# Four graph layers on one core: a stacked inverse transform, two small products moved to GpSimd, and another order of phase three

## The chip, the cores and the metric

The kernel runs on one core of one Trainium2 chip. The metric is the device time of one execution in microseconds (us). An engine is named as the profile names it: PE is TensorE (PEld its weight loads), DVE is VectorE, ACT is ScalarE, POOL is GpSimd, and SP is SyncE, whose queue issues every DMA.

## The reference, cut to what matters

There are 128 graphs of 128 nodes and 128 features, each with a 128 by 128 adjacency matrix. Four layers follow one another, each with a residual and a layer norm at its end. The second is the one that the change is about: a convolution of width 17 along the nodes, messages over learned distances, and a gated recurrent unit.

```python
xc = jnp.transpose(x, (0, 2, 1))
h = relu(bn1(conv1d(xc, conv1_w, 0)))
h = bn2(conv1d(h, conv2_w, 8))                 # 17 taps
x_conv = jnp.transpose(relu(h + xc), (0, 2, 1))
s = x @ w_se.T + b_se                          # 3 codes for each node
A = jnp.exp(-squared_distances(s)) * mask
x_nmp = jnp.einsum('bnm,bmd->bnd', A, relu(x @ w_msg.T + b_msg))
gi = jnp.concatenate([x_conv, x_nmp], -1) @ w_ih.T + b_ih
gh = x @ w_hh.T + b_hh                         # gates r, z, n follow
```

The first layer gathers over the adjacency and has a hidden part of 512 features; the third makes three hops with the row-normalised adjacency; the fourth gathers again and has a hidden part of 256.

## The kernel before

The graphs are worked on in 32 groups of four (`G = 4`), so a tile holds 128 partitions by 4 x 128 numbers and fills one of the eight PSUM banks. There are three phases.

**Phase one** computes the first layer for every group, and the discrete Fourier transform of the second layer's first convolution: 68 frequencies (`SLOTS`), each with a cosine and a sine half, kept in SBUF as `xh`; `wh` holds the transformed taps.

**Phase two** multiplies the two, one frequency after the other: `slot_product` makes three fp32 products for a slot on PE, two slots (a pair) fill a bank, and there are 34 pairs. Even pairs are copied out by ACT and odd ones by DVE into a ring of six tiles (`STAGES`), from which SP stores them to `yh_dram` with at most three stores in flight (`STORES`). POOL negates one half of each slot (`negate`, into `neg_b`). PE may run eight pairs ahead of the copies. The third phase's weights are loaded and split into a high and a low part (`wt_hi`, `wt_lo`) meanwhile.

**Phase three** is a software pipeline that is written out by hand. It has 41 turns (`TURNS3`), and in turn t each engine executes its own list of steps in a fixed order: `stage(step, t - d)` does a step for group t - d if there is such a group. So d is the lag of a step behind the newest group. An engine that waits holds up everything behind it in its list. A step's `until` lines are the semaphores it waits for; PE's `free` lines say which readers must be done with a PSUM bank before it is written again, of which the first that concerns an existing group counts. Since the eight banks are shared by some twenty products, most of the order is about banks.

The steps that matter below are, on PE: `codes` (the points, 16 small products), `distances` (8 small ones), `inverse` (back from 68 frequencies, for each graph one product with 68 rows of cosines and one with 68 rows of sines), `gate_x`, `gate_nmp` and `gate_conv` (each three products of 512 columns in fp32r, high and low parts apart), `hop1` to `hop3`, `y1_t`, `prop_in`, `gather3`, `hidden3` and `down3`. An fp32 product over the four graphs of a group shows as 8 matmul records. On DVE, `agg3` makes `agg3_lo` from the bank that `distances` of the same turn writes next, and `minus_mean` makes minus mean over deviation (`nm`) from 128 x 4 numbers, for `apply2` and `apply3` on ACT. On POOL, `norm` raises 128 x 4 numbers to the power of minus one half. SP's list is `load_x1(t + 2)`, `load_atc(t + 2)`, `load_yh(t + 1)` and `store`; a load waits until the readers of its ring's old entry are done.

The order of PE's turn before is: `codes`, `gather`, `down3` (first half), `messages`, `prop_in`, `down3` (second), `hop3`, `gather3`, `hidden_n`, `gate_x` R and Z, `gate_nmp` R, `distances`, `inverse`, `hop1`, `gate_conv` R, `hidden3` twice, `gate_nmp` N and Z, `gate_conv` N and Z, `y1_t`, `hop2`.

## Time and profile before

| What | us |
|---|---|
| median of 3 runs | 1172.59 |
| lowest and highest | 1169.11, 1173.3 |
| the profiled execution | 1173.6 |
| its span, first to last instruction | 1171.8 |
| PE, DVE, ACT, POOL busy | 1102.7, 833.5, 694.8, 563.0 |

The span is what the rows below divide up. The profiled execution's own time is 1.8 us longer than its span, and 1.0 us above the median. Phase one runs to about 424 us, phase two to about 484, and phase three fills the rest. Merged rows of the timeline overlap a little, as matmuls are pipelined: the distance between the starts of two rows is what a piece of work takes of PE's time.

### The profile page before, as it was taken

How to read it: one execution, taken by the hardware profiler on the slowest of the kernel's cores; microseconds unless marked ns; L12 is line 12 of the kernel's file. 1: busy time of each engine (PE TensorE's matmuls, PEld its weight loads, DVE VectorE, ACT ScalarE, POOL GpSimd, SP SyncE). 2: the span in 40 equal slices, each digit the busy share in tenths (PEclk: the TensorE clock that was granted, in tenths of full speed). 3: DMA queues.
4: the chain of work that ended last, by engine and by line, in shares of the span. 5: the costliest groups of instructions: out<-in, count | busy, mean ns of one | idle time of the engine just before them, and what ended most of it. 6: DMA issues, size and time to landing. Idle time of an engine off the chain costs nothing.

```text
span 1171.8 us, 25210 instructions
## 1 busy us (share of the span) xinstructions
PE 1102.7 (94%) x8267; PEld 990.0 (84%) x8267; DVE 833.5 (71%) x2596; ACT 694.8 (59%) x1296; POOL 563.0 (48%) x524
## 2 busy tenths in 40 slices
PE   7899999999999789899999999999999999999874
PEld 6799999999999679788888888888888888888774
DVE  4477778787777533146887778877787878877974
ACT  4444555555555332256677777767776776767665
POOL 1244433434342235335555555656555565656654
PEclk9999999999999899899999999999999999999998
DMA  4122332223232255411111121211212121220000
GB/s 156 55 64 75 99 91 91 91 91 91 91 91 64 73 168 180 155 50 58 34 40 54 47 65 47 65 38 47 65 47 65 47 65 40 64 65 10 20 28 36
DMA packets 47110, 82.62 MB, mean 71 GB/s; under 512 B 5316, under 2 KB 15368, under 8 KB 46728
## 3 DMA queue, kind: packets, MB, share of 16 engines
q1 hardware_dynamic: 46984, 81.02, 22.5%
q8 instruction: 69, 1.13, 0.4%
q14 instruction: 57, 0.47, 0.1%
HBM read 55.31 MB, written 25.69 MB: 69 GB/s over the span
## 4 chain that ended last, share of the span: by engine, by line
PE 81%; DVE 9%; issue 6%; ACT 2%; DMA 1%; SPq 0%; POOL 0%; DVEq 0%; POOLq 0%; ACTq 0%
PE banks L156 16%; PE banks L465 9%; PE banks L150 9%; PE banks L151 8%; PE banks L152 8%; PE banks L722 4%; PE banks L631 3%; PE banks L632 3%; PE banks L493 3%; PE banks L558 2%; PE banks L609 2%; PE banks L435 2%; DVE stats L1019 2%; DVE prop L1214 2%; PE banks L587 2%
## 5 line engine op out<-in xcount | busy, mean ns | idle before, releaser
L163 POOL TENSOR_TENSOR rstd<-ve,minus_half 128x4 f32<-128x4 f32 x128 | 130.5, 1020 | 101.9 <-DVE ve L1029 98.8
L163 POOL TENSOR_TENSOR r_rms<-ms,minus_half 128x4 f32<-128x4 f32 x32 | 32.3, 1008 | 224.2 <-DVE ms L993 224.2
L465 PE MATMUL banks<-w,s 128*128 128x128 f32 x768 | 101.2, 275 | 0.4 <-DVE y L1007 0.4
L465 PEld LDWEIGHTS banks<-w,s 128*128 128x128 f32 x768 | 95.6, 192 | 3.4 <-issue 0.5
L150 PE MATMUL banks<-agg_hi,w_hi 128*128 128x512 f32 x192 | 82.4, 429 | 10.1 <-issue 8.6
L1373 POOL TENSOR_TENSOR y<-leaky,x_rows 128x512 f32<-128x512 f32 x32 | 42.6, 1331 | 97.3 <-ACT x_rows L922 96.8
L1019 DVE BATCH_NORM_STATS2 stats<-y 128x6 f32<-128x128 f32 x384 | 82.9, 278 | 1.7 <-POOL y L1373 1.6
L1359 POOL TENSOR_TENSOR x3b<-x_rows,late_rows 128x512 f32<-128x512 f32 x32 | 40.9, 1278 | 82.5 <-DVE y L1239 82.5
L160 ACT ACTIVATE agg_hi<-banks 128x512 fp32r<-128x512 f32 x64 | 38.2, 597 | 64.7 <-PE banks L156 36.1
L151 PE MATMUL banks<-agg_lo,w_hi 128*128 128x512 f32 x192 | 76.4, 398 | 0.0
L152 PE MATMUL banks<-agg_hi,w_lo 128*128 128x512 f32 x192 | 76.3, 398 | 0.0
L156 PE MATMUL banks<-at,x_rows 128*128 128x128 f32 x512 | 69.8, 281 | 4.4 <-DVE agg_lo L981 3.0
L156 PE MATMUL banks<-t,atc 128*128 128x128 f32 x512 | 68.8, 278 | 1.3 <-DVE t L1214 1.3
L722 PE MATMUL banks<-w,z 128*128 128x128 f32 x512 | 69.5, 282 | 0.2
L781 ACT ACTIVATE s<-hn,cols 128x512 f32<-128x512 f32 x96 | 65.0, 712 | 7.7 <-DVE hn L1000 7.7
L1000 DVE SCALAR_TENSOR_TENSOR hn<-banks,cols,rv 128x512 f32<-128x512 f32 x96 | 68.2, 736 | 1.0 <-ACT rv L160 0.6
L156 PEld LDWEIGHTS banks<-at,x_rows 128*128 128x128 f32 x512 | 63.9, 196 | 5.3 <-issue 2.9
L722 PEld LDWEIGHTS banks<-w,z 128*128 128x128 f32 x512 | 64.4, 198 | 1.3 <-ACT z L943 1.3
L156 PEld LDWEIGHTS banks<-t,atc 128*128 128x128 f32 x512 | 63.0, 194 | 1.9 <-DVE t L1214 1.9
L1159 DVE SCALAR_TENSOR_TENSOR c_res<-banks,bn_scale,x1c 128x512 f32<-128x512 f32 x32 | 24.0, 751 | 52.0 <-PE banks L632 52.0
L930 ACT ACTIVATE out_rows<-y,nm,rstd 128x128 f32<-128x128 f32 x128 | 52.5, 483 | 11.8 <-DVE nm L1226 11.7
L1315 POOL TENSOR_SCALAR y<-wh 128x128 f32<-128x128 f32 x67 | 34.3, 530 | 47.8 <-ACT xh L160 25.7
(192 smaller groups left out, 3401.1 us busy)
## 6 DMA issues: line engine op xcount, KB each, us to landing
at<-in_at SPq DMA_DIRECT2D x32, 256.0 KB, 2.9
x_rows<-in_x SPq DMA_DIRECT2D x32, 256.0 KB, 2.9
x_scratch<-x SPq DMA_DIRECT2D x32, 256.0 KB, 3.2
ad<-in_ad SPq DMA_DIRECT2D x32, 256.0 KB, 2.7
x1c<-x_scratch SPq DMA_DIRECT2D x32, 256.0 KB, 2.7
atc<-in_at SPq DMA_DIRECT2D x32, 256.0 KB, 2.9
yh<-yh_scratch SPq DMA_DIRECT2D x32, 256.0 KB
out<-out_rows SPq DMA_DIRECT2D x32, 256.0 KB, 3.1
```

Source lines behind the costliest of these rows:

```text
L150: pe.matmul(psum, hi, moving_hi, start=start, stop=False)
L151: pe.matmul(psum, hi, moving_lo, start=False, stop=False)
L152: return pe.matmul(psum, lo, moving_hi, start=False, stop=stop)
L156: last = pe.matmul(psum[:, g, :], lhs(g), rhs(g), start=True, stop=True)
L163: return nc.gpsimd.tensor_tensor(to[:], base[:], minus_half[:], ALU.pow)
L465: last = pe.matmul(bank[7][:, g, :], s[c][:, g, :], w2[:, c, :], start=(c == 0 and g == 0), stop=(c == H0 - 1), skip_group_check=True)
L722: last = pe.matmul(bank[6][:, g, :], z3[c][:, g, :], w32[:, c, :], start=(c == 0 and g == 0), stop=(c == H3 - 1), skip_group_check=True)
L781: nc.scalar.activation(s[c][:], hn[c][:], ACT.Silu, scale=column("rms", c)).then_inc(sem[("s0", "s1", "s2", "s3")[c]], 1)
L930: last = nc.scalar.activation(out_rows[k % OUT_RING][:, g, :], y3[:, g, :], ACT.Identity, bias=nm[1][:, g:g + 1], scale=rstd[3][:, g:g + 1])
L1000: V.scalar_tensor_tensor(out=hn[c][:], in0=bank[(5, 0, 1, 3)[c]][:], scalar=column("b1", c), in1=rv[:], op0=ALU.add, op1=ALU.mult).then_in ...
L1019: last = V.bn_stats(stats[n][:, g, :], y[:, g, :])
L1373: Q.tensor_tensor(y2[:], leaky[:], x2_rows[:], ALU.add).then_inc(sem["y2"], 1)
```

## The change

The **inverse transform** is stacked. The cosines and sines of the first 64 frequencies (`MAIN`) stand in one tile of 128 rows, so that each graph takes one product with 128 rows instead of two with 68. The four frequencies that are left (`REST`, 8 half rows a graph, 32 for the four graphs) are one fp32r product of 512 columns for the whole group: its stationary operand `rest[:, k, :]` stacks high and low parts in four quarters of the partitions, and `rest_idft` holds the matching coefficients.

For that, **phase two** begins with slots 64 to 67. Their two pairs are stored by 16 DMAs, eight a pair, to `rest_dram`; eight times four DMAs (`load_rest`) bring them back into the space of `wt_full`, ACT rounds each eighth (`rest_high`) and DVE subtracts in two quarters (`rest_low`). One more weight is loaded (`rest_idft_full`, 256 KB). The main slots are stored as before. `load_yh` brings the two halves to partitions 0 to 63 and 64 to 127, so its rows are 512 B instead of 1 KB.

**`minus_mean`** leaves DVE for POOL and becomes two instructions there, a negation and a product.

**Phase three** has another order on every engine, other banks, and other lags: the gates' products trail `codes` by two turns instead of one (`gate_x` R stays at one), most of the later steps by one turn more than before, and there are 42 turns. The rings of `x1c` and `atc` have 6 and 11 entries instead of 4 and 8.

Of the order's lists the diff below shows only the new ones.

```diff
-        X1C_RING, ATC_RING, YH_RING, OUT_RING = 4, 8, 2, 2
+        X1C_RING, ATC_RING, YH_RING, OUT_RING = 6, 11, 2, 2
...
-        idft = sb("idft", [SLOTS, 2, P])
+        idft = sb("idft", [P, P])
+        rest_idft_full, rest_idft = sb("rest_idft_full", [P, G * P]), sb("rest_idft", [P, G * P], F32R)
+        rest_full = [wt_full[:, PART * i:PART * (i + 1), :] for i in range(2)]
+        rest = sb("rest", [P, GROUPS, P], F32R)
...
+        SLOT_ORDER = list(range(MAIN, SLOTS)) + list(range(MAIN))
+        NEGATED = [slot for slot in SLOT_ORDER if slot > 0]
+        PARTS = GROUPS // PART
...
+        def stored_pair(engine, p):
+
+            if 0 <= p < REST_PAIRS:
+                engine.wait_ge(rest_stored[p], REST_STORES)
+            elif p >= 0:
+                landed(engine, yh_stored, p - REST_PAIRS)
+
...
-                of_group = yh_dram[:, k * G:(k + 1) * G, :].rearrange("s g (h o) -> s g h o", h=2)
+                of_group = yh_dram.rearrange("s (k g) (h o) -> s k g h o", g=G, h=2)[:, k]
                 to = yh[k % YH_RING]
-                sp.dma_start(to[0:64], of_group[0:64]).then_inc(yh_in[k % YH_RING], 16)
-                sp.dma_start(to[64:SLOTS], of_group[64:SLOTS]).then_inc(yh_in[k % YH_RING], 16)
+                sp.dma_start(to[0:MAIN], of_group[:, :, 0]).then_inc(yh_in[k % YH_RING], 16)
+                sp.dma_start(to[MAIN:P], of_group[:, :, 1]).then_inc(yh_in[k % YH_RING], 16)
...
+                stored_pair(sp, p - STORES)
+                of_pair = spectrum[p % STAGES][:].rearrange("p (s h) o -> p s h o", s=2)
+                slot = SLOT_ORDER[2 * p]
+                if slot < MAIN:
+                    sp.dma_start(yh_dram[slot:slot + 2].rearrange("s b c -> b s c"),
+                                 spectrum[p % STAGES][:].rearrange("p (s a) n -> p s (a n)", s=2)
+                                 ).then_inc(yh_stored[(p - REST_PAIRS) % STORES], 16)
+                else:
+                    for g in range(G):
+                        for s in range(2):
+                            sp.dma_start(rest_dram[g, :, slot - MAIN + s].rearrange("h k o -> k h o"),
+                                         of_pair[g::G, s]).then_inc(rest_stored[p], 16)
+
+            def load_rest(i):
+                if i >= 2:
+                    sp.wait_ge(sem["rest_lo"], 2 * (i - 1))
+                else:
+                    sp.wait_ge(set_dve, DVE_LATE - 1)
+                for r in range(P // (G * REST)):
+                    sp.dma_start(rest_full[i % 2][G * REST * r:G * REST * (r + 1)],
+                                 rest_dram.rearrange("g h s k o -> (g h s) k o")[:, PART * i:PART * (i + 1)]
+                                 ).then_inc(rest_in[i % 2], 16)
...
                 store_slots(p)
+                if p == 8:
+                    for i in range(REST_PAIRS):
+                        stored_pair(sp, i)
+                if p >= 10 and p % 2 == 0 and (p - 10) // 2 < PARTS:
+                    load_rest((p - 10) // 2)
...
                 landed(pe, yh_in, k, 32)
-                free(pe, ("ghn", k - 1), ("y3", k - 8), ("c2_res", k - 1))
+                pe.wait_ge(sem["rest_hi"], k // PART + 1)
+                pe.wait_ge(sem["rest_lo"], 2 * (k // PART + 1))
+                free(pe, ("v", k - 2), ("msg", k - 1), ("z0", k - 9), ("c2_res", k - 1))
+                pe.matmul(flat(bank[7]), rest[:, k, :], rest_idft[:], start=True, stop=False, skip_group_check=True)
                 for g in range(G):
-                    pe.matmul(bank[6][:, g, :], yh[k % YH_RING][:, g, 0, :], idft[:, 0, :], start=True, stop=False)
-                    last = pe.matmul(bank[6][:, g, :], yh[k % YH_RING][:, g, 1, :], idft[:, 1, :], start=False,
-                                     stop=True)
+                    last = pe.matmul(bank[7][:, g, :], yh[k % YH_RING][:, g, :], idft[:], start=False,
+                                     stop=(g == G - 1), skip_group_check=True)
                 last.then_inc(sem["c2_ps"], 1)
...
-            GATE_BANK = {R_GATE: 4, Z_GATE: 7, N_GATE: 0}
+            GATE_BANK = {R_GATE: 1, Z_GATE: 4, N_GATE: 7}
...
                 stage(codes, t)
+                stage(gate_nmp, t - 2, R_GATE)
+                stage(down3, t - 9, 0)
+                stage(messages, t - 1)
+                stage(gate_conv, t - 2, R_GATE)
+                stage(prop_in, t - 5)
+                stage(y1_t, t - 5)
+                stage(down3, t - 9, 1)
+                stage(hidden_n, t - 1)
+                stage(gate_nmp, t - 2, N_GATE)
+                stage(hop2, t - 6)
+                stage(gate_x, t - 2, Z_GATE)
+                stage(gather3, t - 8)
+                stage(gate_conv, t - 2, N_GATE)
+                stage(gate_nmp, t - 2, Z_GATE)
                 stage(gather, t - 1)
+                stage(distances, t)
+                stage(gate_conv, t - 2, Z_GATE)
+                stage(inverse, t)
+                stage(hop3, t - 6)
                 stage(gate_x, t - 1, R_GATE)
+                stage(hop1, t - 5)
+                stage(hidden3, t - 8, 0)
+                stage(hidden3, t - 8, 1)
...
+            def rest_high(i):
+                act.wait_ge(rest_in[i % 2], 16 * 4 * (i // 2 + 1))
+                copy(rest[:, PART * i:PART * (i + 1), :], rest_full[i % 2]).then_inc(sem["rest_hi"], 1)

             for p in range(0, PAIRS, 2):
                 slots_out(p)
+                if p >= 14 and (p - 14) // 2 < PARTS:
+                    rest_high((p - 14) // 2)
                 if p == 6:
...
+                stage(factors, t, 1)
+                stage(hidden3, t - 9, 1)
+                stage(multiple, t - 6, 1)
+                stage(gate_z, t - 3)
+                stage(factors, t, 0)
+                stage(message, t - 1)
+                stage(gate_r, t - 2)
+                stage(gate_n, t - 3)
+                stage(conv_full, t - 1)
+                stage(apply3, t - 10)
+                stage(multiple, t - 6, 0)
+                stage(hidden_n, t - 1)
+                stage(x1_high, t)
+                stage(agg3, t - 8)
+                stage(multiple, t - 5, 3)
+                stage(edges, t)
+                stage(nmp_high, t - 1)
                 stage(conv_high, t - 1)
+                stage(multiple, t - 5, 2)
+                stage(apply2, t - 7)
+                stage(leaky_relu, t - 6)
+                stage(hidden3, t - 8, 0)
...
+            def rest_low(i):
+                dve.wait_ge(sem["rest_hi"], i + 1)
+                for r in (1, 3):
+                    own = slice(G * REST * r, G * REST * (r + 1))
+                    low = rest[own, PART * i:PART * (i + 1), :]
+                    V.tensor_tensor(low, rest_full[i % 2][own], low.bitcast(F32), ALU.subtract
+                                    ).then_inc(sem["rest_lo"], 1)

             for p in range(1, PAIRS, 2):
                 slots_out(p)
+                if p >= 15 and (p - 15) // 2 < PARTS:
+                    rest_low((p - 15) // 2)
                 if p == 7:
...
-            def minus_mean(k, n):
-                until(dve, ("r2", "r3")[n], k)
-                until(dve, ("x3_rows", "out_rows")[n], k - 1)
-                V.scalar_tensor_tensor(out=nm[n][:], in0=mv[2 + n][:, :, 0], scalar=-1.0, in1=rstd[2 + n][:],
-                                       op0=ALU.mult, op1=ALU.mult).then_inc(sem[("nm2", "nm3")[n]], 1)
...
+                stage(twice_n, t - 4)
+                stage(apply1, t - 6)
+                stage(stats2, t - 7)
+                stage(points, t, 0)
+                stage(gate_u, t - 2)
+                stage(stats1, t - 5)
+                stage(moments, t - 7, 2, LN_EPS)
+                stage(moments, t - 5, 1, 4.0 * LN_EPS)
+                stage(points, t, 1)
+                stage(residual3, t - 9)
+                stage(hop, t - 6, 2)
+                stage(scaled_h, t - 5)
+                stage(stats3, t - 9)
+                stage(agg3, t - 8)
+                stage(gate_v, t - 2)
                 stage(nmp_low, t - 1)
                 stage(conv_residual, t)
+                stage(moments, t - 9, 3, LN_EPS)
+                stage(hop, t - 6, 3)
+                stage(twice_x, t - 3)
+                stage(hop, t - 5, 1)
...
+            def minus_mean(k, n):
+                until(pool, ("r2", "r3")[n], k)
+                Q.tensor_scalar(minus_rstd[n][:], rstd[2 + n][:], -1.0, None, ALU.mult
+                                ).then_inc(sem[("minus_r2", "minus_r3")[n]], 1)
+                until(pool, ("minus_r2", "minus_r3")[n], k)
+                Q.tensor_tensor(nm[n][:], minus_rstd[n][:], mv[2 + n][:, :, 0], ALU.mult
+                                ).then_inc(sem[("nm2", "nm3")[n]], 1)
...
+                stage(norm, t - 10, 3)
+                stage(minus_mean, t - 10, 1)
+                stage(residual2, t - 7)
+                stage(add_eps3, t - 8)
+                stage(edge_weights, t - 1)
+                stage(twice_y1, t - 4)
+                stage(norm, t - 5, 1)
+                stage(x1_low, t)
+                stage(norm, t - 7, 2)
+                stage(x3_bias, t - 8)
+                stage(minus_mean, t - 7, 0)
                 stage(conv_low, t - 1)


 def by_group(a):
```

## Rows read from the trace of the kernel before

**Rows 1.** The page's head and its part 1.

```profile
span 1171.8 us, 25210 instructions
...
PE 1102.7 (94%) x8267; PEld 990.0 (84%) x8267; DVE 833.5 (71%) x2596; ACT 694.8 (59%) x1296; POOL 563.0 (48%) x524
```

**Rows 2.** Windows: busy us of each engine, count, clock, DMA share, GB/s.

```profile
1000.00:1100.00 100.00, 97.60 (x729) 86.37 (x728) 81.67 (x289) 71.67 (x138) 59.45 (x50) 1.00 0.14 41
1100.00:1172.00 72.00, 45.90 (x301) 40.75 (x300) 50.08 (x212) 41.65 (x86) 37.25 (x32) 0.89 0.08 30
```

**Rows 3.** Waits of PE, 600 to 1100 us: total, times, longest.

```profile
PE banks L600 <- DVE agg_lo L1232: 14.5, 24, 0.7
```

**Rows 4.** PE timeline, one whole turn: start, length of the merged row.

```profile
1023.03 0.64 PE L587 MATMUL banks<-x1c,code_w 128*32 128x128 f32 x16
...
1032.52 0.39 PE L151 MATMUL banks<-xn_lo,wt_hi 128*128 128x512 f32 x1
1032.75 0.40 PE L152 MATMUL banks<-xn_hi,wt_lo 128*128 128x512 f32 x1
1033.82 0.50 PE L600 MATMUL banks<-points_lr 9*128 9x128 f32 x8 [0.67 <-DVE agg_lo L1232]
1034.25 0.49 PE L631 MATMUL banks<-idft,yh 68*128 68x128 f32 x2
...
1036.14 1.06 PE L156 MATMUL banks<-w3h,atc 128*128 128x128 f32 x8
...
1043.36 0.65 PE L587 MATMUL banks<-x1c,code_w 128*32 128x128 f32 x16
```

**Rows 5.** Groups of 600 to 1100 us: total busy, mean ns.

```profile
L163 POOL TENSOR_TENSOR rstd<-ve,minus_half 128x4 f32<-128x4 f32 x73 | 74.2, 1016 | 48.8 <-DVE ve L1029 48.8
...
L1226 DVE SCALAR_TENSOR_TENSOR nm<-mv,rstd 128x4 f32<-128x4 f32 x50 | 32.8, 656 | 0.0
...
L1214 DVE SCALAR_TENSOR_TENSOR t<-banks,row_inv,w1h 128x128 f32<-128x128 f32 x96 | 27.0, 345 | 0.0
```

**Rows 6.** The page's part 5, the negation on POOL.

```profile
L1315 POOL TENSOR_SCALAR y<-wh 128x128 f32<-128x128 f32 x67 | 34.3, 530 | 47.8 <-ACT xh L160 25.7
```

**Rows 7.** Line 1226 by itself: ns, shortest, median, longest.

```profile
L1226 DVE SCALAR_TENSOR_TENSOR nm<-mv,rstd x64: 143/191/1235, 566.9 to 1167.5; 128x4 f32<-128x4 f32 x64
```

**Rows 8.** PE timeline: first row of turns 0 and 9, of turn 32, and the next.

```profile
485.14 0.65 PE L587 MATMUL banks<-x1c,code_w 128*32 128x128 f32 x16 [1.18 <-DVE prop_w L1138]
...
614.47 0.64 PE L587 MATMUL banks<-x1c,code_w 128*32 128x128 f32 x16
...
1083.76 1.06 PE L156 MATMUL banks<-edge_adj,msg 128*128 128x128 f32 x8
1084.65 1.06 PE L722 MATMUL banks<-w,z 128*128 128x128 f32 x8
```

**Rows 9.** PE and ACT timelines of the last turns.

```profile
1111.29 0.63 PE L672 MATMUL banks<-ident,y 128*128 128x128 f32 x4 [3.54 <-DVE x_rows L1197]
...
1124.85 0.63 PE L672 MATMUL banks<-ident,y 128*128 128x128 f32 x4 [2.45 <-DVE x_rows L1197]
...
1152.70 1.65 ACT L922 ACTIVATE x_rows<-y,nm,rstd 128x128 f32<-128x128 f32 x4 [1.87 <-POOL x3b L1359]
...
1167.68 1.65 ACT L930 ACTIVATE out_rows<-y,nm,rstd 128x128 f32<-128x128 f32 x4 [3.66 <-DVE nm L1226]
```

**Rows 10.** SP's own queue in phase two.

```profile
427.67 0.43 SPq L384 DMA_DIRECT2D msg_w<-in_msg  x1
...
437.71 1.72 SPq L376 DMA_DIRECT2D yh_scratch<-s  x3
```

**Rows 11.** PE and ACT timelines at both ends of phase two.

```profile
424.32 0.46 PE L556 MATMUL banks<-wh,xh 128*128 128x128 f32 x2 [0.58 <-ACT xh L160]
...
483.69 0.27 PE L576 MATMUL banks<-ident,prop_rows 128*128 128x128 f32 x1
...
437.72 0.60 ACT L160 ACTIVATE hn<-banks 128x512 f32<-128x512 f32 x1 [4.17 <-DMA yh_scratch<-hn]
```

More of the change, by code:

```diff
@@ L297, in everything_second @@
             engine.wait_ge(sem["neg_b"], SLOTS - 1)
-            for p in range(PAIRS - STORES, PAIRS):
-                landed(engine, yh_stored, p)
+            for p in list(range(REST_PAIRS)) + list(range(PAIRS - STORES, PAIRS)):
+                stored_pair(engine, p)
         @block.sync
@@ L408, in _ @@
                     stage(load_yh, t + 1)
-                stage(store, t - 9)
+                stage(store, t - 10)
             for i in range(OUT_RING):
@@ L893, in hidden_n @@
                 until(act, "u", k - 1)
-                nc.scalar.activation(ghn[:], bank[6][:], ACT.Identity, bias=half_bhn[:], scale=0.5
+                nc.scalar.activation(ghn[:], bank[2][:], ACT.Identity, bias=half_bhn[:], scale=0.5
                                      ).then_inc(sem["ghn"], 1)
@@ L1327, in _ @@
             Q.memset(pick[:].bitcast(F32), 1.0).then_inc(set_pool, 1)
-            for slot in range(6, SLOTS):
-                negate(slot)
+            for i in range(5, SLOTS - 1):
+                negate(i)
             def x1_low(k):
@@ L1449, in layouts @@
     share = np.where(slot == 0, 1.0, 2.0) / L
+    inverse = waves(node).transpose(1, 2, 0) * share[:, None, None]
+    rest_idft = np.zeros((4, G, REST, G, P), np.float32)
+    for g in range(G):
+        rest_idft[:, g, :, g, :] = inverse[MAIN:].transpose(1, 0, 2).reshape(REST, P)
+    rest_idft = rest_idft.reshape(P, G * P)
     return {
```

225 lines of the change are left out of this document (82 added, 143 removed).

## The prediction

> **What bounds the kernel now.** I read the page's shares first [rows 1]: PE is busy 94% of the span, the others 48 to 71%. The windows by stage then show where that is not so [rows 2]: between 1000 and 1100 us PE is busy 97.60 of 100 us, and in the last 72 us only 45.90. So the middle of phase three goes by PE's own work, the end by latency. PE's waits over 500 us of it hold a single entry [rows 3]: `distances` for `agg3_lo` of DVE, 24 times, 0.60 us each. No load and no other engine stands in that list. The timeline of one turn gives the sizes [rows 4]: a turn takes 1043.36 - 1023.03 = 20.33 us. The last `gate_nmp` product starts at 1032.75 and gives way after 0.23 (the step from the row before it), yet `distances` starts at 1033.82, so 0.84 us pass, some 0.1 to 0.2 of them for changing to small products. I put the wait at 0.70. `inverse` has 1036.14 - 1034.25 = 1.89 us. The 23 turns from turn 9 to turn 31 took (1083.76 - 614.47) / 23 = 20.40 us each, spells of lower clock included [rows 8].
>
> **The change, part by part.**
>
> Inverse transform: for each graph two products of 128 columns become one, and 512 columns in fp32r are added. Four graphs of one fp32 product each take 1084.65 - 1083.76 = 0.89 us [rows 8] and an fp32r product 0.23 [rows 4], so 1.12 instead of 1.89. Some 0.1 of the 1.89 is the lead after the small products, which now falls on another step. I take a saving of 0.67 a turn (0.77 at most; not under 0.5, since eight products leave and five come).
>
> Wait for `agg3_lo`: in the new lists I walked through one turn, with `codes` at 0, PE's pieces back to back at the sizes above, and the other engines' lists at their own durations. The wait was there because `agg3` came late in DVE's list, before a step of PE's middle. Now `gather3` starts at 9.3 and `distances` at 12.5. ACT's high part is done at 11.1. DVE starts `hop` 2 at 8.9 (four pieces of 0.345 [rows 5]), then `scaled_h`, `stats3` and `agg3` follow and end at 12.0. That leaves some 0.3 us. The second tight place is `gather3`, which waits until ACT has copied `ghn` out of its bank: behind `message` (after `messages`, 3.4) stand `gate_r`, `gate_n`, `conv_full`, `apply3` (1.65 us [rows 9]), `multiple` and `ghn`, done at 9.0 against 9.2. Everything else has over 0.5 us: `codes` of the next turn wants `prop` at 19, done at 17.5; `gather` wants `edge_adj` at 11.6, done at 3.3. I remove the whole 0.70 and put 0.12 back for the two tight places, between nothing and 0.75. The turn is 20.40 - 0.67 - 0.70 + 0.12 = 19.15 us. ACT and DVE, 14.5 and 16.5 us of work a turn [rows 2], fit in it.
>
> `minus_mean`: DVE loses two instructions a turn, 0.656 us in the mean [rows 5], though it waits for PE anyway. The same line takes 0.143 to 1.235 us [rows 7]; a length so unequal for 512 numbers is waiting within the instruction. The Trainium skill, page "SBUF — State Buffer", section on its two separate sides, says that VectorE with two SBUF inputs and GpSimd hold a shared port pair by turns, for a whole instruction. By that rule the trace agrees, and moving work to GpSimd blocks other DVE steps (`twice_n`, `twice_x`, `gate_u`) in its place. From rows, one such block costs 1.235 - 0.143 = 1.1 us; two at the head of DVE's list delay `points` and `gate_u`, but `hop` 2 still starts about when PE delivers, since DVE idled before it. POOL gains four small instructions a turn. The trace has none like them: below stands 0.14, DVE's own [rows 7], above the power on as many numbers, 1.02 [rows 5]. The negation of 128 x 128 in 0.53 [rows 6] is nearest, and I take 0.5. POOL then has 12.1 + 2.0 us of a turn (59.45 over 100 us are 12.1 [rows 2]), so this costs nothing in the middle. In the drain it lies on the path (below). The Trainium skill, page "GPSIMD Engine Reference", section 3.1, speaks against the move: VectorE stays the rule for elementwise work, GpSimd being 1.96 times as slow. Worked out from that ratio, an estimate is 0.28 an instruction, by which the sum below would be some 2 us less.
>
> Phase two: PE's work is the same, (483.69 - 424.32) / 34 = 1.75 us a pair [rows 11]. The first negation is needed a little earlier: 0.3 us. SP has 14 more stores at the start and one more weight load, at 0.43 to 0.57 each [rows 10] 7 us. Pair 6 was copied at 437.72, after a store had landed [rows 11]. PE had it ready at 436.5 and wants its bank for pair 14 at 448.8. So the copy may be some 10 us later, and the stores hide there; with that cover gone each us counts (0 to 5). The 32 `load_rest` DMAs take SP 15 us over the 14 pairs that last 24.5, beside 8 for stores, and the handshakes lag by some 3 us behind copies that have six tiles. The extra copies on ACT (0.6) and DVE (two of 0.7) a second pair lie in their gaps.
>
> Rings: SP's loads no longer wait for readers of the same turn. No PE wait was a load's, so nothing. `load_yh` has as many DMAs as before.
>
> Fill: before, turns 0 to 8 took 614.47 - 485.14 = 129.3 us [rows 8]. Since the gates now come two turns behind, the early turns are lighter. With fp32 steps at 0.89, fp32r ones at 0.70, `codes` 0.67, `distances` 0.53, `messages` 1.12, the turns are 7.5 and 8 (latency), three of 10.6, 12.8, two of 14.6, and 16.9: 106.2 us, 23 less.
>
> Drain: the same work comes back here. Before, from 1083.76 to the end 88.0 us. After, turn 32 has 19.0 less `codes`, `distances` and `inverse`, 16.6; turn 33 also lacks `messages`, `hidden_n`, `gather` and `gate_x`, 13.2. Then a chain sets the pace: `y1_t`, statistics, two powers, `x3b`, two small POOL instructions, `apply2`, `leaky_relu`, `hidden3`, `down3`. I add it up to 11.5 us, three times (before, 1124.85 - 1111.29 = 13.6 [rows 9]), then 9 and 7.1 to the end of the last `apply2`. From there it took 1171.8 - 1154.4 = 17.4 [rows 9]; with the small instructions 18. Sum 98.4, 10 more.
>
> **Sum**: 485.4 + 106.2 + 23 x 19.15 (440.5) + 98.4 = 1130.5 of span; with the 1.8 us around it 1132.3. The profiled execution, 1173.6, is 1.0 above the median, so **1131** for the median of runs.
>
> **The rivals.**
>
> The wait moves: one of the two tight places, or one I misjudged, costs 0.75 us a turn, as `agg3_lo` did. Over 31 turns 0.63 more than I put back is 20 us: 1151. For it: three tenths of a us are less than my walk can promise, and shared-port blocks fall on DVE. Against: only the excess over the slack counts.
>
> Fill and drain better than I add up: if the drain stays at its old 88 us and no tight place costs (3 us), 1118. Against it: two more steps on POOL, and one more turn.
>
> Phase two stalls: stores or `load_rest` fall behind PE by more than the ten us of cover, 5 to 10 us: 1139. Against it: the queue catches up in 3 us after its worst wait before.
>
> The other side: POOL becomes the bound. The small instructions would have to cost over (20.4 - 12.1) / 4 = 2.1 us each to bring the turn back to 20.4 and the time to about 1172, and 2.3 would give some 1190. The power on as many numbers, 1.02, speaks against it. Only twice that decides.
>
> **How the numbers follow.** Forecast as summed 0.58, the wait moves 0.22, better ends 0.09, phase two 0.05, POOL 0.06. The predicted time is 1131. The range 1114 to 1160 leaves out POOL and the worse half of the moved waits. Under 0.5% (6 us) this kernel's runs can't be told from no change; the first four cases are all faster by more, save the far tail of the second: faster 0.89, same 0.05, slower 0.06.
>
> **What would show it.** `inverse` as one fp32r product and four fp32 ones, 1.1 us in all. The starts of `codes` 19.0 to 19.3 us apart, and no wait at `distances`; waits at `gather3` for `ghn` or at `distances` for `agg3_lo` would be the second case. The small POOL instructions near 0.5 us. No PE idle time in phase two. Turn 9 starting near 592, turn 32 near 1032. The prediction is wrong if PE idles over 0.5 us a turn at any place, or if phase three's last ten turns take over 110 us.

## The result, and the profile after

The changed kernel took 1131.81 us in the median of four runs (1130.30 to 1132.04), the kernel before 1170.85 in the same comparison. The ratio is 0.9655, with an interval of 0.9628 to 0.9682. The forecast was 1131 us. The profiled execution took 1131.74 us, with a span of 1129.9. The forecast had taken the profiled execution to lie 1.0 us above the median, as it did before; it lay 0.1 below it.

The page's head and part 1 after, against [rows 1]:

```profile
span 1129.9 us, 24862 instructions
...
PE 1074.6 (95%) x8043; PEld 961.1 (85%) x8043; DVE 818.6 (72%) x2549; ACT 709.2 (63%) x1305; POOL 613.6 (54%) x652
```

PE has 224 matmuls and 28 us of busy time less, but the span shrank by 42, so 14 us of PE's idle time went as well. The windows after, against [rows 2]:

```profile
600.00:800.00 200.00, 200.00 (x1508) 175.67 (x1507) 161.33 (x576) 156.12 (x293) 142.11 (x148) 1.00 0.17 54
800.00:1000.00 200.00, 200.00 (x1515) 175.44 (x1514) 162.36 (x577) 158.05 (x298) 142.32 (x148) 1.00 0.17 55
...
1060.00:1100.00 40.00, 32.00 (x229) 28.62 (x230) 36.35 (x157) 29.26 (x57) 28.74 (x34) 0.96 0.06 21
1100.00:1130.00 30.00, 14.52 (x93) 11.65 (x91) 13.39 (x61) 15.65 (x34) 16.20 (x24) 0.92 0.12 44
```

From 600 to 1000 us PE is busy for the whole of both windows; before, the 100 us in the middle of [rows 2] had 97.60. The list of PE's waits between 590 and 1030 us is empty; from 600 to 1100 us before it had 24 of them at 0.60 us [rows 3]. In 1060 to 1100 us it is DVE that is nearly full: 36.35 of 40 us.

One turn of PE's timeline after, against [rows 4]:

```profile
802.59 0.64 PE L637 MATMUL banks<-x1c,code_w 128*32 128x128 f32 x16
...
811.90 1.05 PE L160 MATMUL banks<-at,x_rows 128*128 128x128 f32 x8
...
815.18 0.50 PE L650 MATMUL banks<-points_lr 9*128 9x128 f32 x8
...
816.41 0.39 PE L682 MATMUL banks<-rest_idft,rest 128*128 128x512 f32 x1
816.65 1.05 PE L684 MATMUL banks<-idft,yh 128*128 128x128 f32 x8
817.53 1.06 PE L160 MATMUL banks<-t,atc 128*128 128x128 f32 x8
...
821.52 0.65 PE L637 MATMUL banks<-x1c,code_w 128*32 128x128 f32 x16
```

A turn is 821.52 - 802.59 = 18.93 us. `inverse` is the fp32r product and four fp32 ones, 817.53 - 816.41 = 1.12 us. `gather3` starts 9.31 us into the turn and `distances` 12.59, as the walk through the lists had it (9.3 and 12.5).

The turn that [rows 4] shows is not quite a typical one. More first rows of turns before, and two windows of 3 us:

```profile
634.70 0.64 PE L587 MATMUL banks<-x1c,code_w 128*32 128x128 f32 x16
...
656.68 0.65 PE L587 MATMUL banks<-x1c,code_w 128*32 128x128 f32 x16
...
921.85 0.65 PE L587 MATMUL banks<-x1c,code_w 128*32 128x128 f32 x16
...
942.09 0.64 PE L587 MATMUL banks<-x1c,code_w 128*32 128x128 f32 x16
...
648.00:651.00 3.00, 3.00 (x13) 2.71 (x12) 1.93 (x6) 2.18 (x4) 2.52 (x3) 0.50 0.20 79
791.50:794.50 3.00, 3.00 (x13) 2.71 (x12) 1.79 (x6) 2.18 (x4) 2.52 (x3) 0.50 0.24 72
```

Of the 22 distances between the first rows of turns 9 to 31, 15 are 20.21 to 20.24 us, five are 20.27 to 20.38, and two are 21.98 and 21.99. In each of these two turns the granted clock fell to 0.50, that is 1.2 GHz, for a few microseconds (last column but two of the windows), at a cost of 1.75 us. A clean turn before is therefore 20.24 us, and the mean of 20.40 that the prediction started from holds 0.16 of slower and disturbed turns.

The first rows of turns 0, 9 and 31 and the first `down3` of turn 32, against [rows 8]. Turn 32 has no `codes`; it starts at 1010.85 + 18.93 = 1029.78:

```profile
485.30 0.64 PE L637 MATMUL banks<-x1c,code_w 128*32 128x128 f32 x16 [1.27 <-DVE prop_w L1209]
...
594.36 0.65 PE L637 MATMUL banks<-x1c,code_w 128*32 128x128 f32 x16
...
1010.85 0.65 PE L637 MATMUL banks<-x1c,code_w 128*32 128x128 f32 x16
...
1030.39 1.05 PE L774 MATMUL banks<-w,z 128*128 128x128 f32 x8
```

So phase three divides into a fill (turns 0 to 8), 23 full turns (9 to 31), of which the table has the mean, and a drain. The same division serves for every experiment, from the profile of each; it leaves phases one and two out, whose end wanders between 483.4 and 489.9 us from profile to profile.

| Kernel | phase three | fill | one turn | drain |
|---|---|---|---|---|
| before | 686.7 | 129.3 | 20.40 | 88.0 |
| forecast | 645.1 | 106.2 | 19.15 | 98.4 |
| changed | 644.6 | 109.1 | 18.93 | 100.1 |
| changed, second profile | 643.9 | 109.1 | 18.93 | 99.4 |
| 1: new order, old inverse | 665.6 | 115.6 | 19.59 | 99.4 |
| 2: old order, stacked inverse | 660.0 | 122.3 | 19.61 | 86.7 |
| 3: old kernel, `agg3` earlier | 670.5 | 128.6 | 19.59 | 91.4 |
| 4: old order, stacked, `agg3` earlier | not read | | | |
| 5: `minus_mean` on DVE | 648.0 | 109.2 | 18.93 | 103.4 |
| 6: POOL's two steps swapped | 644.8 | 109.3 | 18.93 | 100.1 |
| 7: another order in the last turns | 648.0 | 109.6 | 18.93 | 103.0 |
| 8: `agg3` later | 651.7 | 109.7 | 19.22 | 100.1 |
| 9: `ghn` later | 656.1 | 111.3 | 19.35 | 99.8 |
| 10: shorter rings | 645.0 | 109.4 | 18.93 | 100.1 |
| 11: as 4, `agg3` earlier in the middle only | 643.2 | 121.0 | 18.93 | 86.8 |

The profiled execution of experiment 4 had a mean granted clock of 0.56, against 0.98 to 0.99 in all the others, and its times compare with none of them.

### The profile page after: what moved, and what is told of

Read it like the earlier page. It is cut to its first block, busy times and chain, and to the rows that moved or that the text cites. A ratio compares the mean times of both kernels' runs of the same rounds, so it can differ in the third digit from the quotient of the medians.

```text
span 1129.9 us, 24862 instructions
## 1 busy us (share of the span) xinstructions
PE 1074.6 (95%) x8043; PEld 961.1 (85%) x8043; DVE 818.6 (72%) x2549; ACT 709.2 (63%) x1305; POOL 613.6 (54%) x652
## 4 chain that ended last, share of the span: by engine, by line
PE 89%; DVE 4%; issue 3%; POOL 2%; ACT 1%; DMA 1%; SPq 0%; ACTq 0%; DVEq 0%; POOLq 0%
PE banks L160 18%; PE banks L154 12%; PE banks L155 10%; PE banks L156 10%; PE banks L515 10%; PE banks L774 4%; PE banks L684 3%; PE banks L543 3%; PE banks L608 3%; PE banks L659 2%; PE banks L485 2%; PE banks L637 2%; PE banks L575 1%; PE banks L611 1%; PE banks L613 1%
## 5 line engine op out<-in xcount | busy, mean ns | idle before, releaser
L1420 POOL TENSOR_TENSOR y<-ya,yb 128x512 f32<-128x512 f32 x32 | 41.6, 1299 | 63.2 <-PE banks L724 62.5
L1406 POOL TENSOR_TENSOR x_lo<-x1c,x_hi 128x512 fp32r<-128x512 f32 x32 | 41.2, 1287 | 62.7 <-ACT x_hi L164 62.7
L1223 DVE TENSOR_TENSOR xn_lo<-banks,xn_hi 128x512 fp32r<-128x512 f32 x32 | 22.1, 692 | 60.4 <-ACT xn_hi L164 60.4
L1387 POOL TENSOR_SCALAR y<-wh 128x128 f32<-128x128 f32 x67 | 38.0, 585 | 44.4 <-ACT xh L164 25.7
L1426 POOL TENSOR_TENSOR xc_lo<-xc,xc_hi 128x512 fp32r<-128x512 f32 x32 | 41.1, 1285 | 34.0 <-issue 17.5
```

The costliest lines, as they stand in the source:

```text
L1406: Q.tensor_tensor(x1_lo[k % 2][:], x1c[k % X1C_RING][:], x1_hi[k % 2][:].bitcast(F32), ALU.subtract).then_inc(sem["x1_lo"], 1)
L1420: Q.tensor_tensor(y1[:], ya[:], yb[:], ALU.subtract).then_inc(sem["y1"], 1)
```

## The experiments

Times are medians of four runs or more, and each ratio is to the kernel before in runs on the same chip. Experiments 1 to 4 ran on one chip, 5 to 7 with the changed kernel again on a second, 8 to 10 on a third, and 11 on a fourth, so across these sets the ratios compare better than the times.

### 1. The new order with the old inverse transform

Everything of the change but the stacked transform and its part of phase two:

```diff
-                pe.matmul(flat(bank[7]), rest[:, k, :], rest_idft[:], start=True, stop=False, skip_group_check=True)
                 for g in range(G):
-                    last = pe.matmul(bank[7][:, g, :], yh[k % YH_RING][:, g, :], idft[:], start=False,
-                                     stop=(g == G - 1), skip_group_check=True)
+                    pe.matmul(bank[7][:, g, :], yh[k % YH_RING][:, g, 0, :], idft[:, 0, :], start=True, stop=False)
+                    last = pe.matmul(bank[7][:, g, :], yh[k % YH_RING][:, g, 1, :], idft[:, 1, :], start=False,
+                                     stop=True)
```

> The changed kernel, with the inverse transform and phase two of before (two products of 68 rows for each graph, no rest), on the new order and banks. Theory (PE's own work sets the turn): the turn grows from 18.93 by the 0.67 us of the products, 32 times 21 us, so about 1153 us, turns 19.6 us apart, no PE wait in the middle. Rival (the new order alone made the gain, the products lay in its slack): 1132 to 1137 us. Rival (phase two's extra stores and loads cost something that this gives back): below 1149 us.

Measured: 1152.69 us, ratio 0.9824 (0.9795 to 0.9854). Turns of 19.59 us, and PE waits for nothing from 600 to 1000 us. The drain is 99.4 us. With the old transform the new order still has no wait, so its 11 longer us of drain belong to the order and not to the transform.

### 2. The old order with the stacked transform

The other half: the kernel before with the stacked transform, its phase two and its extra loads, nothing else.

> The kernel before, with the stacked inverse and its phase two only; order, banks, lags, rings and minus_mean as before. Theory (PE's own work sets the turn, and the wait at distances lies ahead of the inverse in the turn): 0.67 us a turn less, 21 us in all, about 1150 us; the wait for agg3_lo stays at 0.6 us, the turn goes from 20.24 to 19.57. Rival (a cycle through DVE sets the turn and the wait grows by what is saved): 1166 to 1171 us, wait over 1.0 us.

Measured: 1150.17 us (1144.42 to 1151.61), ratio 0.9792 (0.9758 to 0.9826). PE's waits from 600 to 1000 us keep one entry, as [rows 3] had:

```profile
PE banks L650 <- DVE agg_lo L1303: 12.5, 21, 0.7
```

It is 0.60 us a turn, as before, with turns of 19.61 in the mean and 19.57 in the median. The transform is worth 0.67 us a turn here (20.24 less 19.57, clean turns on both sides). In the new order it is worth 19.59 less 18.93, 0.66. So its worth doesn't hang on the order around it.

Phase two takes 59.6 us from its first product to the one behind its last, here as in the changed kernel, and 59.4 before. PE has no wait within it. With 14 stores more at its head and 32 `load_rest` DMAs, SP kept up.

### 3. The old kernel with `agg3` earlier on DVE

One step moved by two places, in a list of the kernel before:

```diff
+                stage(agg3, t - 7)
                 stage(minus_mean, t - 6, 0)
                 stage(stats3, t - 8)
-                stage(agg3, t - 7)
```

> The kernel before with one line moved: on DVE agg3 stands ahead of minus_mean and stats3 instead of behind them. Theory (the wait was only a matter of agg3's place in DVE's list): agg3_lo is done some 1.6 us earlier, the wait at distances goes, 0.6 to 0.7 us in some 25 turns, so 15 to 17 us less, about 1155 us, turns of 19.6 us. Rival (another wait of PE takes its place, since stats3 and the points now come later): 1166 to 1171 us.

Measured: 1157.81 us, ratio 0.9869 (0.9845 to 0.9894). The turns are 19.59 us and the wait is gone, so it cost 20.24 less 19.59, 0.65 a turn. But the drain grew from 88.0 to 91.4 us. In the last turns `agg3` now goes ahead of `minus_mean` and waits for ACT first:

```profile
1126.83 0.69 DVE L1232 TENSOR_TENSOR agg_lo<-banks,agg_hi 128x512 fp32r<-128x512 f32 x1 [0.27 <-ACT agg_hi L160]
1127.44 0.15 DVE L1226 SCALAR_TENSOR_TENSOR nm<-mv,rstd 128x4 f32<-128x4 f32 x1
```

That this is what lengthens the drain is tested in experiment 11.

### 4. Both

> Both: the kernel before with the stacked inverse and with agg3 moved ahead on DVE. Theory (the new order buys that one wait and no more, and shifts work from the fill to the drain without gain): 21 and 16 us add up, about 1134 us, within 4 us of the changed kernel; turns of 18.9 us. Rival (with shorter turns the old order has further waits that only the new one avoids): 1140 to 1155 us, with PE waits in the middle.

Measured: 1138.57 us, ratio 0.9697 (0.9666 to 0.9727). The 4.6 us over the 1134 expected are about the drain's 3.4 of experiment 3. By the ratios (0.9697 here, 0.9655 and 0.9677 of the changed kernel, with intervals that overlap) one step moved and the new transform have all but 2 to 5 us of what the change has. What then do the new order, its lags, banks and rings give?

### 5. `minus_mean` back on DVE

```diff
         @block.vector
+            def minus_mean(k, n):
+                until(dve, ("r2", "r3")[n], k)
+                until(dve, ("x3_rows", "out_rows")[n], k - 1)
+                V.scalar_tensor_tensor(out=nm[n][:], in0=mv[2 + n][:, :, 0], scalar=-1.0, in1=rstd[2 + n][:],
+                                       op0=ALU.mult, op1=ALU.mult).then_inc(sem[("nm2", "nm3")[n]], 1)
...
                 stage(gate_u, t - 2)
+                stage(minus_mean, t - 10, 1)
...
+                stage(minus_mean, t - 7, 0)
                 stage(conv_residual, t)
```

The two steps of the same name are taken out of POOL's list.

> The changed kernel with minus_mean back on DVE as one instruction (behind gate_u for group t - 10, ahead of conv_residual for group t - 7). Theory (it is off PE's path in the middle, and in the drain it costs DVE about what it cost POOL): 1130 to 1135 us, turns still 18.93. Rival (a block of up to 1.2 us by POOL on each of the two eats the small slack ahead of distances and gather3): PE waits come back, 1140 us or more.

Measured: 1136.21 us, ratio 0.9697 (0.9669 to 0.9724); the changed kernel in the same comparison 1132.13, ratio 0.9677 (0.9650 to 0.9705). The intervals overlap. The middle is the same, 18.93. The profile has a drain of 103.4 us against 100.1 and 99.4, and its timeline from 1100 us to the end says from what:

```profile
1108.22 2.05 PE L774 MATMUL banks<-w,z 128*128 128x128 f32 x16 [1.18 <-ACT z L1002]
...
1109.76 0.42 DVE L1297 SCALAR_TENSOR_TENSOR nm<-mv,rstd 128x4 f32<-128x4 f32 x1
...
1110.22 1.65 ACT L989 ACTIVATE out_rows<-y,nm,rstd 128x128 f32<-128x128 f32 x4 [1.47 <-DVE nm L1297]
...
1114.29 0.76 PE L154 MATMUL banks<-agg_hi,w_hi 128*128 128x512 f32 x1 [2.89 <-issue]
...
1115.88 1.24 DVE L1297 SCALAR_TENSOR_TENSOR nm<-mv,rstd 128x4 f32<-128x4 f32 x1 [1.13 <-POOL rstd L167]
...
1116.99 3.50 PE L774 MATMUL banks<-w,z 128*128 128x128 f32 x16
```

The same place in the second profile of the changed kernel:

```profile
1106.28 2.05 PE L774 MATMUL banks<-w,z 128*128 128x128 f32 x16 [1.10 <-ACT z L1002]
...
1106.70 1.64 ACT L989 ACTIVATE out_rows<-y,nm,rstd 128x128 f32<-128x128 f32 x4
...
1110.92 0.47 PE L154 MATMUL banks<-agg_hi,w_hi 128*128 128x512 f32 x1 [1.46 <-ACT agg_hi L164]
```

In DVE's list `nm` stands behind the statistics of another group, so `apply3` (`out_rows`) starts 2.00 us after `down3` instead of 0.42. `residual3` and `agg3_lo` come later with it, and PE is idle for 2.89 us ahead of `hidden3` instead of 1.46. That is 1.4 us of the edit's own cost. The rest is the clock: right behind that idle time the granted clock is 0.50, and the next `down3` takes 3.50 us where the others take 2.05. Whether the longer idle time brought the lower clock isn't shown. DVE also stands idle 1.13 us before `nm` while POOL makes its power, three times in the last turns.

The runs don't confirm a cost. The four runs of this kernel with a mean clock of 0.984 to 0.991 and the five of the changed one with 0.986 to 0.992 agree once they are put side by side by clock: at 0.986, 1136.05 and 1136.38 us against 1135.59 and 1135.79; at 0.991, 1131.97 against 1131.96 and 1132.13. So the move to POOL is worth between nothing and some 1.4 us, all of it in the drain, and no gain clear of the noise is shown.

### 6. POOL's `minus_mean` ahead of `x3_bias`

```diff
-                stage(x3_bias, t - 8)
                 stage(minus_mean, t - 7, 0)
+                stage(x3_bias, t - 8)
```

> The changed kernel with minus_mean ahead of x3_bias in POOL's list. Theory (in the last turns the chain to apply2 passes x3_bias, 1.27 us): the middle is the same, the last five turns or so get shorter, 2 to 5 us less, about 1128 us. Rival (DVE, busy 91% there, sets those turns): under 1 us.

Measured: 1131.72 us, ratio 0.9663 (0.9641 to 0.9685), so no gain. The rows of one of the last turns:

```profile
1101.68 0.20 POOL L1367 TENSOR_TENSOR nm<-minus_rstd,mv 128x4 f32<-128x4 f32 x1
1101.83 1.27 POOL L1431 TENSOR_TENSOR x3b<-x_rows,late_rows 128x512 f32<-128x512 f32 x1
...
1103.22 1.65 ACT L981 ACTIVATE x_rows<-y,nm,rstd 128x128 f32<-128x128 f32 x4 [2.17 <-POOL x3b L1431]
```

`nm` is there at 1101.88, 1.3 us before ACT starts `apply2`, and `apply2` now waits for `x3b` instead. There is a single tile of `x3_rows`: it can't be written before `x3_bias` has read the group before. I had overlooked that reader. Both orders have the same two steps ahead of `apply2`.

### 7. Another order in the last turns

This is the kernel of experiment 6, with POOL's two steps swapped, and with one thing more: in turns 39 to 41 (`LAST` is 39) PE does `gather3` first, and ACT and DVE do `agg3` before `multiple` and `residual3`. PE's and DVE's part, against the changed kernel:

```diff
+                if t >= LAST:
+                    stage(gather3, t - 8)
                 stage(codes, t)
...
-                stage(gather3, t - 8)
+                if t < LAST:
+                    stage(gather3, t - 8)
...
+                if t >= LAST:
+                    stage(agg3, t - 8)
                 stage(residual3, t - 9)
```

> As the one before, and in the last three turns gather3 ahead of down3 on PE and agg3 earlier on ACT and DVE. Theory (group 31's gather3 stood 2.5 us behind down3 of group 30): another 2 us less, about 1126 us. Rival (the last chain goes by other steps): no change against the one before.

Measured: 1135.24 us, ratio 0.9696 (0.9670 to 0.9723), no gain over experiment 6 (1131.72, 0.9663), and by the profile's drain (103.0 us against 100.1) a loss. The rows:

```profile
1111.76 1.24 ACT L1006 ACTIVATE z<-banks,cols 128x512 f32<-128x512 f32 x2
1111.77 1.26 POOL L1447 TENSOR_TENSOR at<-atc,eps_ident 128x512 f32<-128x512 f32 x1
...
1113.14 1.13 PE L160 MATMUL banks<-at,x_rows 128*128 128x128 f32 x8 [1.96 <-issue]
1114.11 3.44 PE L775 MATMUL banks<-w,z 128*128 128x128 f32 x16
...
1121.55 1.65 ACT L993 ACTIVATE out_rows<-y,nm,rstd 128x128 f32<-128x128 f32 x4 [1.73 <-POOL nm L1377]
1123.32 0.69 DVE L1311 TENSOR_TENSOR y<-banks,x3b 128x512 f32<-128x512 f32 x1 [3.53 <-ACT out_rows L993]
```

`down3` has its input soon after ACT starts the first `z`: in the second profile of the changed kernel it starts 0.72 us behind it (1113.68 and 1112.96). Here it starts 2.35 us behind, at 1114.11, because `gather3` now stands ahead of it in PE's list and waits for POOL's `at`. So the edit costs 1.6 us on the chain at this point. Another 1.4 us are that `down3` at a lower clock, which again comes right behind idle time of PE. What `gather3` gains is lost: `agg3` is done early, but the last `residual3` waits for `apply3` of the group before, which must have read the one tile `y3`, and that `apply3` comes from the `down3` that was put off. By clock, its run at 0.991 took 1133.26 us against 1131.96 and 1132.13 of the changed kernel, and the one at 0.986 took 1135.52 against 1135.59 and 1135.79. So by the runs the edit costs about 1 us at most, and gains nothing.

### 8. `agg3` behind `gate_v` on DVE

```diff
-                stage(agg3, t - 8)
                 stage(gate_v, t - 2)
+                stage(agg3, t - 8)
```

> The changed kernel with agg3 behind gate_v on DVE, so 0.6 us later. Theory (0.3 to 0.4 us of slack there, as the prediction had it): a PE wait of 0.2 to 0.35 us before distances comes back in every full turn, 6 to 10 us in all, about 1139 us. Rival (the slack is larger than read, or the wait is made up elsewhere in the turn): no change.

Measured: 1137.59 us, ratio 0.9709 (0.9676 to 0.9742). The turn is 19.22 us, 0.29 more, for a step that holds DVE 0.6 us ahead of `agg3_lo` (in the changed kernel `agg3_lo` starts at 813.82 and the step behind it at 814.41). So `distances` had some 0.3 us to spare. PE's waits from 600 to 1000 us:

```profile
PE banks L650 <- issue: 4.5, 21, 0.4
```

The wait is back at the same product, `distances`, though the profile names no engine for it.

### 9. ACT's `ghn` later

A copy of a whole tile that nobody reads is put before `hidden_n` on ACT:

```diff
+            def idle_copy(k):
+                copy(unused[:], wt_full[:, 0:G, :])
+
...
+                stage(idle_copy, t - 1)
                 stage(hidden_n, t - 1)
```

> The changed kernel with one more ACT copy of a full tile (0.6 us, into a tile that nobody reads) ahead of the copy of ghn. Theory (0.2 to 0.3 us of slack before gather3): PE waits 0.3 to 0.6 us before gather3 in every full turn, 9 to 18 us in all, about 1145 us. Rival (ACT makes it up, or gather3's bank is released in time): no change.

Measured: 1140.61 us, ratio 0.9726 (0.9694 to 0.9759). From turn 10 on the turns are 19.37 us, 0.44 longer, and the copy puts `ghn` off by 0.52 us (it starts at 819.15, `ghn` at 819.67), so `gather3` had only 0.1 to spare. PE's waits from 610 to 1000 us name the one that the prediction named:

```profile
PE banks L160 <- ACT ghn L957: 4.2, 20, 0.2
```

They are 0.21 us each, less than the 0.44, since idle time counts from the modelled end of the row before, and PE's rows overlap: in the changed kernel the row ahead of `gather3` starts at 811.67 and is 0.40 long, while `gather3` starts at 811.90.

### 10. Rings of 5 and 9

```diff
-        X1C_RING, ATC_RING, YH_RING, OUT_RING = 6, 11, 2, 2
+        X1C_RING, ATC_RING, YH_RING, OUT_RING = 5, 9, 2, 2
```

> The changed kernel with rings of 5 and 9 entries for x1c and atc instead of 6 and 11. Theory (loads have a turn to spare, so that SP may wait for readers of the same turn): no change, 1132 us. Rival (SP, held up by atc's readers into the next turn, issues yh too late): PE waits for yh before inverse, 1140 us or more.

Measured: 1130.93 us, ratio 0.9654 (0.9620 to 0.9687): no difference, with turns of 18.93 and no wait in the middle. Entries above 5 and 9 are worth nothing. Whether the new lags would run well with the old 4 and 8 wasn't tried.

### 11. The old order, stacked transform, `agg3` earlier in the middle only

Experiments 3 and 4 lost in the drain what `agg3` ahead of `minus_mean` costs there. So the step is moved only while there are new groups, in the kernel of experiment 2:

```diff
+                if t < GROUPS:
+                    stage(agg3, t - 7)
                 stage(minus_mean, t - 6, 0)
                 stage(stats3, t - 8)
-                stage(agg3, t - 7)
+                if t >= GROUPS:
+                    stage(agg3, t - 7)
```

> The kernel before with the stacked inverse, and agg3 moved ahead on DVE in the first 32 turns only; in the last nine it stands where it stood. Theory (the old order with these two edits runs its middle at 18.93 us a turn as the changed kernel does, and its drain stays at 88 us or so): turns of 18.93 us without a PE wait, 1133 to 1136 us. Rival one (a wait of the old order remains in the middle): turns of 19.1 us or more, 1138 us or more. Rival two (the early agg3 did not lengthen the drain): the same time as with agg3 ahead in all turns, 1138.6 us, and a drain of over 90 us.

Measured: **1129.86 us** in the median of five runs (1128.91 to 1131.29), ratio 0.9640 (0.9624 to 0.9656), the changed kernel having 0.9655 (0.9628 to 0.9682) and 0.9677 (0.9650 to 0.9705) in its two comparisons. Its windows:

```profile
600.00:800.00 200.00, 200.00 (x1519) 175.50 (x1518) 161.93 (x595) 154.11 (x297) 125.57 (x107) 1.00 0.19 57
800.00:1000.00 200.00, 200.00 (x1499) 174.88 (x1498) 162.81 (x590) 153.93 (x297) 125.78 (x106) 1.00 0.19 55
...
1060.00:1100.00 40.00, 27.62 (x188) 24.96 (x187) 34.34 (x144) 25.49 (x52) 23.21 (x20) 0.91 0.06 21
```

Here, too, PE has no idle time in 400 us, and the turn is 18.93 us, the same as the changed kernel's to the hundredth. The fill is 121.0 us instead of 109.1 and the drain 86.8 instead of 100.1, in all 643.2 us against 644.6. It is at least as fast as the changed kernel, from two edits. Against experiment 4 (0.9697, 0.9666 to 0.9727) the intervals don't touch, and the two differ in the last nine turns alone: so it was the earlier place of `agg3` in these turns that lengthened the drain in experiments 3 and 4.

## Why the prediction held, step by step

The sum was 1130.5 us of span and 1129.9 was measured. The terms were not that good: their errors cancel, start -0.1, fill +2.9, the 23 turns -5.1, drain +1.7. What held is the mechanism, PE's own work and one wait in the middle and a shift from fill to drain; that the sum came within a microsecond is luck.

**The turn.** Forecast 20.40 - 0.67 - 0.70 + 0.12 = 19.15 us, measured 18.93. This is the term that was most off, 5.1 us over 23 turns. Against the clean turn of 20.24 us, experiment 3 gives 0.65 for the wait, put at 0.70, and experiments 2 and 1 give 0.67 and 0.66 for the transform, put at 0.67. The two terms that were mis-sized are others. The start of 20.40 held 0.16 of slower turns, most of it the two spells of 1.2 GHz, that the changed kernel's middle doesn't have. And the 0.12 put back for tight places cost nothing. Together these are 0.28 a turn, less 0.05 for the wait. From 600 to 1000 us of the changed kernel the granted clock was 1.00 throughout, while the kernel before had 0.98 in two windows of 100 us. Why it had such spells is open: experiment 2, with the wait still there, also has 1.00 in these windows, so the wait doesn't bring them every time.

**The two tight places.** Both are where the forecast had them. The timeline of all engines in the turn shown above:

```profile
810.94 0.68 ACT L953 ACTIVATE ghn<-banks,half_bhn 128x512 f32<-128x512 f32 x1
...
813.82 0.67 DVE L1297 TENSOR_TENSOR agg_lo<-banks,agg_hi 128x512 fp32r<-128x512 f32 x1
```

`ghn` is done at 811.62 for a `gather3` at 811.90, and `agg3_lo` at 814.49 for `distances` at 815.18. The delays of experiments 8 and 9 give what was to spare: 0.3 us at `distances` and 0.1 at `gather3`, less than the 0.69 and 0.28 between these ends and starts. They also show what the rival, the wait moving, would have cost: half a microsecond on one engine made phase three 7 and 11 us longer. It was a close thing, and a chance of 0.22 was not too much.

**`minus_mean` on POOL.** The four small instructions were put at 0.5 us each; they are shorter. Groups from 600 to 1000 us, of the changed kernel:

```profile
L1437 POOL TENSOR_TENSOR at<-atc,eps_ident 128x512 f32<-128x512 f32 x21 | 36.5, 1736 | 0.0
...
L1257 DVE SCALAR_TENSOR_TENSOR yb<-tz,nn 128x512 f32<-128x512 f32 x21 | 25.6, 1219 | 0.0
L1364 POOL TENSOR_SCALAR minus_rstd<-rstd 128x4 f32<-128x4 f32 x42 | 16.4, 391 | 1.8
...
L1367 POOL TENSOR_TENSOR nm<-minus_rstd,mv 128x4 f32<-128x4 f32 x42 | 8.4, 200 | 3.5
```

They are 0.39 and 0.20, 1.2 us a turn in all instead of 2.0, far from the 2.1 each from which POOL would have been the bound. That it costs nothing in the middle held. The small loss put on the drain isn't there: the part behind the last `apply2`, put at 18 us instead of 17.4, took 17.2 (from 1112.7). The profile of experiment 5 points the other way, since on DVE the step stands behind others and cost 1.4 us. That was not foreseen.

**Blocks between DVE and POOL.** The prediction expected new ones at the head of DVE's list. There is one pair: `yb` takes 1.219 us (before 0.692) and `at` 1.736 (before 1.335). One turn shows how:

```profile
802.03 1.29 POOL L1445 TENSOR_TENSOR y<-leaky,x_rows 128x512 f32<-128x512 f32 x1
...
802.66 1.21 DVE L1257 SCALAR_TENSOR_TENSOR yb<-tz,nn 128x512 f32<-128x512 f32 x1
...
803.28 1.74 POOL L1437 TENSOR_TENSOR at<-atc,eps_ident 128x512 f32<-128x512 f32 x1
```

`yb` starts while POOL's `y` runs, stays until that is over at about 803.3, and then needs its own 0.5 to 0.6; `at` starts at 803.28 and is 0.40 longer than before. So they take turns, each for a whole instruction. By the rule of the Trainium skill, page "SBUF — State Buffer", section on the two separate sides, which gives the shared port pair to one of them for an instruction at a time, the trace agrees. It is not `minus_mean`'s doing: with `minus_mean` back on DVE (experiment 5) `at` still takes 1.740 us and `yb` 1.029, and in experiment 11, which has the old order, 1.285 and 0.694. The new order brings the two together, for in experiment 1, with the old transform, they take 1.216 and 1.733. Since DVE has time to spare in the middle, it costs nothing there. What the prediction took as evidence for such blocks, `nm` of 0.656 us on DVE, also went with the order alone: 0.153 us in experiment 5.

**Fill.** 109.1 us against 106.2. Half of the miss is turn 5, forecast at 12.8 and measured at 14.3: `distances` waits in it, once.

```profile
543.58 0.50 PE L650 MATMUL banks<-points_lr 9*128 9x128 f32 x8 [1.22 <-issue]
```

It is the first turn with the steps of lag five. Turn 4 took 0.9 us more than forecast (0.48 of it one wait for `msg`) and turn 1 took 1.0 less. The rest is 0.2 us in each of the six others, probably from changes between product forms, which I had left out in summing single pieces; no run shows that.

**Drain.** 100.1 us against 98.4. The three turns that I put at 11.5 us took 12.2, 13.2 and 11.0; what follows them, put at 9, 7.1 and 18, came out 0.6 us shorter. A spell of 1.2 GHz from 1081 us on is in the second of the three; the second profile, with the same waits of PE around it (1.05 and 0.90 us) and no such spell, has 12.2, 12.0 and 11.5 and a drain of 99.4. The chain was the one described, but in these turns DVE's load counts as well as latency: 36.35 of 40 us.

**Phase two.** Nothing, as forecast: the phase ends at 483.75 us and `codes` starts at 485.30, before 483.69 and 485.14 [rows 8, 11].

**What the parts are worth.** Stacked transform: 26.7 us of phase three by itself, 686.7 to 660.0, of which 3.5 are the two spells of lower clock before; the medians of the runs, 1173.80 and 1150.17 us, are 23.6 apart. The wait: 16.8 more, 660.0 to 643.2, with one DVE step in another place. The rest of the new order, the lags, the banks, the longer rings and `minus_mean` on POOL: minus 1.4, between profiles that differ by 0.7 when one kernel is profiled twice. This rest makes the fill 11.9 us shorter and the drain 12.6 to 13.4 longer. That it is the longer lags that do this is argued, from the steps that each early and late turn holds; no run changes the lags alone. The prediction saw this give-and-take (23 less in the fill, 10 more in the drain) but laid the 23 to the lags and lighter products together; 8.3 of the 20.2 us that were measured come with the old lags too, as experiment 11 shows.

## What to carry to other kernels

In a pipeline in which one engine is full, an engine's own work and its single repeated wait are the whole gain in the middle; find the one step whose place causes the wait and move that before a new order is written, for here the rest of the new order only made the fill shorter and the drain longer by about as much. Give the steady turns and the last turns orders of their own where a step that helps the one stands on the other's chain. Before a step is moved to shorten a chain, list all readers of the tile that it lets be written, since in experiment 6 a tile with one copy took the gain, and list what then stands behind the step in its own engine's list, since in experiments 3, 5 and 7 that was a step of the chain.

## What the runs showed of the hardware

Within the runs of one kernel, the mean granted clock of each run goes with most of what differs: in the five runs of the changed kernel in the second comparison 1130.5 us went with 0.992, 1132.0 and 1132.1 with 0.991, 1135.6 and 1135.8 with 0.986. That is some 0.7 us for each thousandth of clock here; from 0.985 to 0.995 the runs of experiment 10 give 0.5. So edits of a few microseconds are best compared at about equal clocks. It is a rough scale: two runs of the kernel before at 0.986 took 1169.81 and 1171.75 us. The lower clock showed up within single products of the drain, 16 `down3` matmuls in 3.44 us instead of 2.05 in experiment 7, where PE had been idle for 1.96 us just before the eight products ahead of them, and 3.50 us in experiment 5 behind 2.89 us of idle time. Idle time alone doesn't decide it: of the changed kernel's two profiles, with the same waits of PE around 1080 us, one has a spell of 1.2 GHz there and the other none. From 600 to 1000 us only the profiles of the kernel before and of experiment 4 had a window below 1.00; experiments 2, 8 and 9, whose PE waited there too, had none.

A GpSimd instruction on 128 x 4 numbers was far cheaper than the power on as many: 0.20 us for a product of two tiles and 0.39 in the mean (0.23 to 0.62) for a product with a constant, against 1.03 for the power. The Trainium skill, page "GPSIMD Engine Reference", section 3.1, would have VectorE do such elementwise work, being 1.96 times as fast; here DVE did the two together in 0.15 us undisturbed, against 0.59 in the mean on POOL, a larger ratio, and yet the middle of the kernel took the same 18.93 us a turn, because neither engine was the bound there.
